# Two cross attentions on one core: scores computed two tiles ahead instead of three, exponentials moved to the head of ScalarE's step

## The reference

```
x = x + cross_attention_0(layernorm(x), ctx)
x = x + quantised_ffn(layernorm(x))
x = x + cross_attention_1(layernorm(x), ctx)   # with LoRA, and 4 tokens with keys and values of their own
x = x + mixture_of_experts(layernorm(x))       # 8 experts, top 2
```

## Time and profile before

| What | us |
|---|---|
| Median of 3 runs | 1635.89 |
| Lowest and highest | 1633.92, 1649.41 |
| The profiled execution, its own time | 1650.75 |
| Its span, first to last instruction | 1649.0 |
| First attention, first norm to last statistics | 90.3 to 314.4 |
| Second attention, first norm to last statistics | 819.5 to 1058.1 |

### The profile page before, as it was taken

How to read it: one execution, slowest core, us unless ns; L and a number is a source line. 1 busy time by engine, 2 the same in 40 slices (tenths; PEclk the granted TensorE clock), 3 DMA queues, 4 the chain that set the end, 5 groups by cost and what they waited for, 6 DMA issues and landing times. The chain is left out here.

```text
span 1649.0 us, 29274 instructions
## 1 busy us (share of the span) xinstructions
PE 1289.7 (78%) x8795; PEld 955.6 (58%) x8796; DVE 1064.8 (65%) x1954; ACT 796.7 (48%) x1146; POOL 522.8 (32%) x427
## 2 busy tenths in 40 slices
PE   5859999538986009799879999663079999999996
PEld 3427777434432008646446767553068999899995
DVE  4947777585589875544758888662346666665663
ACT  0536565244499777100567878563034334443342
POOL 1037777200000000100066767347403323333333
PEclk9979999868999559855899999855589999999998
DMA  5000000100033542100013222374323222222221
GB/s 196 1 4 1 0 0 0 58 1 1 0 150 136 204 158 68 40 1 0 23 45 91 64 89 64 92 251 156 113 62 53 37 51 46 45 47 44 47 43 12
DMA packets 62636, 102.67 MB, mean 62 GB/s; under 512 B 9648, under 2 KB 50704, under 8 KB 61936
## 3 DMA queue, kind: packets, MB, share of 16 engines
q1 hardware_dynamic: 48272, 84.98, 15.8%
q0 software_dynamic: 14304, 16.93, 5.7%
HBM read 65.79 MB, written 37.92 MB: 63 GB/s over the span
## 5 line engine op out<-in xcount | busy, mean ns | idle before, releaser
L1876 POOL DMA_INDIRECT out<-ex_yo,ex_mt x78 | 136.3, 1747 | 316.0 <-DVE ex_yo L1851 181.6
L1753 PE MATMUL ex_ps_h<-ex_xT_hi,a_arena 128*128 128x256 f16 x1248 | 212.4, 274 | 0.0
L1795 ACT ACTIVATE ex_hT<-ex_ps_h,e_b1T,e_unscale 128x256 f32<-128x256 f32 x312 | 150.8, 564 | 115.4 <-PE ex_ps_h L1753 115.4
L609 PE MATMUL at_ps_y<-c_VW,at_pT_hi 128*128 (+1 forms) x1024 | 172.3, 274 | 1.3 <-DVE main_x_res L736 1.3
L1753 PE MATMUL ex_ps_h<-ex_xT_lo,a_arena 128*128 128x256 f16 x624 | 170.9, 274 | 0.0
L1766 PE MATMUL ex_ps_y<-e_w_lo,ex_hT_hi 128*128 x624 | 170.1, 273 | 0.0
L1766 PE MATMUL ex_ps_y<-a_arena,ex_hT_lo 128*128 x624 | 170.1, 273 | 0.0
L1766 PE MATMUL ex_ps_y<-a_arena,ex_hT_hi 128*128 x624 | 170.1, 273 | 0.0
L811 POOL TENSOR_TENSOR at_sc<-at_sc,at_ri 128x960 f32<-128x960 f32 (+1 forms) x96 | 127.5, 1342 | 86.9 <-DVE at_ri L731 86.6
L811 POOL TENSOR_TENSOR at_sc<-at_sc,at_mx 128x960 f32<-128x960 f32 (+1 forms) x96 | 127.4, 1342 | 44.2 <-DVE at_mx L708 44.0
L609 PE MATMUL at_ps_y<-c_VW,at_pT_lo 128*128 (+1 forms) x512 | 140.0, 273 | 0.0
(11 more groups left out here) (295 smaller groups left out, 2982.0 us busy)
## 6 DMA issues: line engine op xcount, KB each, us to landing
at_half<-in_L_ffn_W SPq DMA_DIRECT2D x32, 512.0 KB, 4.3
up_scratch<-gm_stg SPq DMA_DIRECT2D x16, 768.0 KB, 3.2
gm_stg<-up_scratch SPq DMA_DIRECT2D x16, 768.0 KB, 4.2
ex_row<-xs SPq DMA_DIRECT2D x39, 260.0 KB, 2.7
rt_stage<-in_L_ffn_W SPq DMA_DIRECT2D x16, 512.0 KB, 4.2
main_x_res<-in_x SPq DMA_DIRECT2D x8, 512.0 KB, 12.7
out<-main_x_res SPq DMA_DIRECT2D x4, 1024.0 KB, 12.5
xs<-rt_pad SPq DMA_DIRECT2D x18, 130.0 KB
```

The lines of the kernel that those rows point to most:

```text
L609: last = nc.tensor.matmul(ps_y[:, 0:D], a[j][:, n, :], b[:, bass.ds(off + n * D, D)], start=(n == 0 and i == 0), stop=(n == NP - 1 and i = ...
L1753: last = nc.tensor.matmul(ps_h[:, n, :], a[:, bass.ds(e * WN + d * HID + n * P, P)], b[:, d, :], start=(m == 0), stop=(m == 3 * DT - 1))
L1795: last = nc.scalar.activation(hT[:, n, :], ps_h[:, n, :], ACT.Relu, bias=b1T[:, bass.ds(e * HT + n, 1)], scale=unscale[:, 0, bass.ds(e, 1)])
L1876: nc.gpsimd.indirect_dma_start(out=acc[:, :], out_offset=bass.IndirectOffsetOnAxis(ap=mt[j][:, q, 1:2].bitcast(U32), axis=0), in_=yo[j][:, ...
```

## The change

In the attention function, on all engines, the scores (with take_scores, maxima and subtract) are made two tiles ahead of the step's probabilities, not three, and the turn of x, norm, high_x, rest_x and add_bias three ahead, not four. The lead passed to `in_steps_by` goes from 4 to 3. On ScalarE `exps` goes from a place behind `high_p` (for tile k + 2) to the head of the step (for tile k + 1). Sums, inverses, normalise, turn_probs, high_p, rest_p, output, residual and statistics keep their indices. The counts that `column_sums` and `total` wait for follow. It applies to both attentions.

```
@@ TensorE
-                need(pe, xhi_r, NS * e + 7 if not isinstance(e, int) else min(NS * e + 7, NT))
-                need(pe, xlo_r, NS * e + 7 if not isinstance(e, int) else min(NS * e + 7, NT))
+                need(pe, xhi_r, NS * e + 6 if not isinstance(e, int) else min(NS * e + 6, NT))
+                need(pe, xlo_r, NS * e + 6 if not isinstance(e, int) else min(NS * e + 6, NT))
...
-                if there(k + 3, NT):
-                    scores(k + 3, (j + 3) % 2)
+                if there(k + 2, NT):
+                    scores(k + 2, j % 2)
                 if experts_w and j == 3 and there(k, NT):
                     column_sums(k // NS)
-                if there(k + 4, NT):
-                    turn_x(k + 4, j % 2)
+                if there(k + 3, NT):
+                    turn_x(k + 3, (j + 1) % 2)
...
-            in_steps_by(nc.tensor, NT, 4, 1, NS, step)
+            in_steps_by(nc.tensor, NT, 3, 1, NS, step)
@@ ScalarE
-                if there(k + 4, NT):
-                    norm(k + 4, j % 2)
+                if there(k + 1, NT):
+                    exps(k + 1, (j + 1) % NS)
                 if there(k + 3, NT):
-                    take_scores(k + 3, (j + 3) % NS)
-                if there(k + 4, NT):
-                    high_x(k + 4, j % 2)
+                    norm(k + 3, (j + 1) % 2)
+                if there(k + 2, NT):
+                    take_scores(k + 2, (j + 2) % NS)
+                if there(k + 3, NT):
+                    high_x(k + 3, (j + 1) % 2)
                 if there(k, NT):
                     high_p(k, j % 2)
-                if there(k + 2, NT):
-                    exps(k + 2, (j + 2) % NS)
                 if experts_w and there(k, NT):
                     weights(k // NS, j)
...
-            in_steps_by(nc.scalar, NT, 4, 0, NS, step)
+            in_steps_by(nc.scalar, NT, 3, 0, NS, step)
@@ VectorE
-                if there(NS * e + 7, NT):
-                    dve.wait_ge(xhi_r, NS * e + 8)
+                if there(NS * e + 6, NT):
+                    dve.wait_ge(xhi_r, NS * e + 7)
...
-                if there(k + 3, NT):
-                    maxima(k + 3, (j + 3) % NS)
+                if there(k + 2, NT):
+                    maxima(k + 2, (j + 2) % NS)
...
-                if there(k + 4, NT):
-                    rest_x(k + 4, j % 2)
+                if there(k + 3, NT):
+                    rest_x(k + 3, (j + 1) % 2)
...
-            in_steps_by(nc.vector, NT, 4, 2, NS, step)
+            in_steps_by(nc.vector, NT, 3, 2, NS, step)
@@ POOL
                 if there(k + 1, NT):
                     normalise(k + 1, (j + 1) % NS)
+                if there(k + 2, NT):
+                    subtract(k + 2, (j + 2) % NS)
                 if there(k + 3, NT):
-                    subtract(k + 3, (j + 3) % NS)
-                if there(k + 4, NT):
-                    add_bias(k + 4)
+                    add_bias(k + 3)
...
-            in_steps_by(nc.gpsimd, NT, 4, 0, NS, step)
+            in_steps_by(nc.gpsimd, NT, 3, 0, NS, step)
```

## The result

| | before | after |
|---|---|---|
| Median of 3 runs, us | 1635.89 | 1672.93 |
| Lowest and highest | 1633.92, 1649.41 | 1672.83, 1674.77 |
| Profiled execution, us | 1650.75 | 1674.77 |
| First attention, first norm to end of last statistics | 90.31 to 314.40, 224.1 | 90.05 to 328.11, 238.1 |
| Between the two | 505.1 | 504.5 |

The ratio of the medians is 1.021 (95% interval 1.012 to 1.029, so 20 to 48 us): slower by 37.0 us. The forecast was 1675. The two attentions became longer by 14.0 and 25.4, 39.4 together; 39.1 had been worked out. Some executions of one and the same kernel take 12 to 15 us longer (of the 22 of the kernel before beside experiments 3, 6, 7 and 8 two took 1648.61 and 1649.02, the others 1633.62 to 1637.97), and of before the 1649.41 and the profiled execution are such.

What follows compares the result with a forecast made beforehand. A closed loop through POOL's order was taken to replace TensorE's 6.30 us step as the bound; +13.4 (first attention) and +25.7 (second) sum to +39.1 on 1635.9, giving 1675 us, range 1655 to 1700.

Steps and rivals of the forecast that it cites:

- The ring: Both attentions: closed loop from one tile's subtract to the next's; 6.85 us a step in the first, 0.55 over TensorE's step.
- 0.12 for both: In the loop: releases POOL to ScalarE and ScalarE to VectorE cost 0.12 us together, with 0 and 0.28 as ends.
- First attention: +13.4 predicted: First attention: last exponentials 15.5 us later, at 315.6; the tail of 12.2 behind them gives back 2.1.
- I cost it at nothing: TensorE's clock: low stretches behind seven long gaps lose 1.8 us of work each, covered by slack in the following steps.
- low clock inside the attentions: Sign that would show the forecast wrong: a low TensorE clock within the attentions in the profile after.
- Second attention: +25.7 predicted: Second attention: rounds of four steps take 30.98 us instead of 27.29; last exponentials +28.1, with 2.4 given back behind them.
- the price is in the loop already: ScalarE: norm and turn_x are waited for behind the exponentials' new wait, but add nothing beyond the loop's length.
- TensorE's wait for norm: First attention: TensorE waits about 0.55 us a step for norm ahead of each turn_x, the whole excess, once.
- The clock as a rival: Second attention: TensorE at low clock a whole step behind seven long gaps, +28, in all +67, 1703 us; 8 in 100.
- The table load: First attention: the exponentials' table load of 1.28 us falls into idle time before the first exps; otherwise 1.3 us once.
- it lies in nothing that I changed: Base: the 15 us between profiled execution and the other runs' median lies outside the changed code; forecast uses the median.
- The fallback: First attention: if the loop vanished, the two-step chain of 12.64 us would remain, 6.32 a step, no cost.

Runs made afterwards that it cites:

- experiment 3: Changed kernel with two extra 128 x 128 additions on POOL in each step, behind add_bias: 1677.08 us in one run.
- experiment 6: The change in the first attention only, the second as in the kernel before: ratio 1.0075 to the kernel before.
- experiment 7: Changed kernel with only ScalarE's norm moved, to tile k+4 behind high_p: 1682.24 us in one run.
- experiment 8: Changed kernel with POOL's subtract ahead of normalise and norm moved to tile k+4 behind high_p: median 1644.06 us, ratio 1.0062 to the kernel before.
- experiment 1: Changed kernel with POOL's subtract put ahead of its normalise: median 1654.92 us, ratio 1.0065 to the kernel before.
- experiment 2: Changed kernel with normalise on eight of the 16 heads only, for timing alone as results differ: 1641.63 us in one run.
- experiment 4: Kernel before, scores still three ahead, with exps(k+2) moved to the head of ScalarE's step, ahead of norm: 1654.70 us in one run.
- experiment 9: Kernel before, scores still three ahead, with exps(k+2) moved to second place of ScalarE's step, behind norm(k+4): ratio 1.0008 to the kernel before.
- experiment 5: Changed kernel with exps(k+1) moved back behind high_p(k) on ScalarE, POOL as in the change: 1905.81 us in one run.

## Why the prediction was right

**The ring.** "subtract(t), exps(t), sums(t) and inverses(t), normalise(t), subtract(t+1)" is the bound: 6.77 measured, 6.85 predicted. Experiments 1 and 2 open and shorten it and the step falls to 6.35 to 6.38 and 6.30; experiments 3 and 7 change POOL's load and norm's place and it stays 6.76. The terms: exps to sums 1.19 (1.17 and a release had been put in), sums to normalise 1.78 as taken, normalise to subtract 1.86 (1.88 taken), subtract to exps 1.94. The last is 1.90 and a release of 0.04, and that of ScalarE to VectorE is within 0.04 too: 0.12 for both was on the high side of what came out, near the lower end that had been kept.

**First attention: +13.4 predicted, +14.0 measured,** but two terms were mis-sized and cancel: that the sum came so close is luck. The last exponentials came at 312.23, not 315.6, mostly because the ring is 0.08 shorter over 28 tiles. The tail behind them was to be 12.2 and took 15.9. Turn_probs came 4.92 behind the exponentials, as said; then the transposes took 1.97 instead of the 0.87 that I had put in. The rows of the two are from the timeline and the windows (columns as above):

```profile
317.15 1.97 PE L598 MATMUL at_ps_p<-main_ident,at_sc 128*128 128x128 f32 x8 [3.05 <-POOL at_sc L811]
```

```profile
316.00:318.00 2.00, 0.85 (x4) 0.85 (x5) 1.08 (x3) 0.00 (x0) 1.10 (x1) 0.53 0.00 0
318.00:320.00 2.00, 2.00 (x12) 1.63 (x11) 0.90 (x2) 1.20 (x2) 0.00 (x0) 0.50 0.00 0
```

TensorE had been idle for 3.05 us in front of turn_probs, because the distance of two leaves it nothing else to do at the end, and the clock then stood at its 1.2 GHz level for some six microseconds. Before, it stayed at 1.00 through this tail. "I cost it at nothing" holds for the steps and not for the tails. Experiments 3 and 7 give the price, as they have the same steps and the same gap of 3.05 there: with about half as much low clock the tail took 14.4, with none 13.1. So 2.8 of the 3.7 us are the clock, and the first attention is 11.1 us longer than before where the clock stays up (experiment 7), 14.0 where it falls. The "low clock inside the attentions" was one of the prediction's own signs of being wrong; it came, in the tails alone.

**Second attention: +25.7 predicted, +25.4 measured.** The steps came as worked out: 8.35, 7.83, 7.27 and 7.27 for 8.42, 7.88, 7.34 and 7.34, each 0.05 to 0.07 shorter for the releases, and 30.73 for 30.98. Counted from the first norm, the last exponentials came 26.3 later than before, where 28.1 had been worked out; the tail was 15.1 for 13.5, behind a gap of 3.43 with the clock at 0.50 (in experiment 3, behind the same gap at 1.00, it took 13.4). Here too two misses cancel. How the +25 is made up: opening POOL's ring gives back 16.1 (experiment 1). The 9.3 that stay have the step of 8.36 in them, in which high_w stands between two exponentials. The prediction had that step, at 8.42, beside the ring. Norm behind the exponentials, which costs 9.8 with scores three ahead (experiments 4 and 9), gives nothing back with two ahead (experiments 7 and 8), as "the price is in the loop already" said.

**TensorE's wait for norm.** Foretold as "0.55 a step, the whole excess". The rows say 0.24 for the matmul and 0.73 for its weight load, and the step is 0.46 longer. As a sign it was right; experiment 7 shows that it was never the cause, as the argument by the ring had said.

**The clock as a rival.** It would have put TensorE at the low level for a whole step behind each long gap. Behind the gaps of 1.33 and 1.82 read above it was at 1.00. The two tails had it low behind 3.05 and 3.43, but the length of a gap does not settle it. The same places in experiment 7 (first tail) and experiment 3 (second tail, where L598 is L600), with the stretch behind each:

```profile
329.49 1.09 PE L598 MATMUL at_ps_p<-main_ident,at_sc 128*128 128x128 f32 x8 [3.05 <-POOL at_sc L811]
```

```profile
330.00:332.00 2.00, 2.00 (x21) 1.83 (x20) 1.13 (x2) 1.09 (x2) 0.00 (x0) 1.00 0.00 0
```

```profile
1089.45 1.09 PE L600 MATMUL at_ps_p<-main_ident,at_sc 128*128 128x128 f32 x8 [3.43 <-POOL at_sc L813]
```

```profile
1090.00:1092.00 2.00, 2.00 (x20) 1.83 (x19) 1.17 (x2) 1.09 (x2) 0.00 (x0) 1.00 0.00 0
```

In experiment 5 it was low behind 3.18 and at 1.00 behind 3.10 one step on (207.68). The Trainium skill, "TensorE: Matmul & The Clock Gate", section "HAM oscillation — how this bites in real kernels", lets each burst behind such a wait start slow. That did not happen in the steps of this kernel; it happened in the two tails and in every second step of experiment 5's first attention, and not in the two places above.

**The table load** at the first exponentials was to be hidden, and was: it starts at 99.04 and takes 1.28, and the exponentials start at 102.00, where POOL releases them.

**The base.** Sum and median are to be set against each other with care. The profiled executions differ by 24.0: +14.0, +25.4, -0.6 between the attentions and -14.5 behind them, in code that the change does not touch. The stretch behind the second attention took 590.9 in the profiled run of before and 574.9 to 585.0 in all the others. Such time can lie elsewhere too: in the profiled runs of experiments 1 and 7 the first norm came at 102.8 and 102.5, in all the others at 89.6 to 91.0. What makes it was not found. That "it lies in nothing that I changed" fits these lengths, and taking it out of the base was right; 1635.9 + 39.4 is 1675.3, and 1672.93 was measured.

**The fallback** of 6.32 a step for the chain over two steps, should the ring vanish: experiment 1 had 6.35 to 6.38, experiment 2 6.30.

## What to carry to other kernels

Before work is moved closer together across engines, follow each item from its first instruction round to the same instruction of the next item, through every queue order, and add up the durations: a ring longer than the bounding engine's step is the new step, and no share of busy time shows it. An engine that is a third busy (POOL) can be in that ring by order alone. Then work of its own outside the ring costs next to nothing (experiment 3), while turning round two of its instructions (a step of 6.76 becomes 6.35) or shortening the one inside the ring (6.30) counts. When an instruction is put at the head of a queue, look for the one behind it that somebody waits for already, here norm, and keep that one in front.

## What the runs showed that had not been expected

- The place of one instruction decides between 6.8 and 9.5 to 11.1 us a step: with scores two tiles ahead, the exponentials behind high_p close a ring through the low part of x (1905.81 us in all, experiment 5).
- The same gap of TensorE can leave the granted clock at either level: behind 3.05 us it was 0.53 in the kernel after and 1.00 in experiment 7, behind 3.43 it was 0.50 and, in experiment 3, 1.00; behind 2.19 it was 0.59 in the kernel before, behind 2.23 (at 896.37 in experiment 7) 1.00. What decides was not found. In the first tail it is worth 2.8 us.
- A release from POOL to ScalarE costs 0.04 us (208.90 + 1.90 to 210.84), less than the 0.14 from VectorE to ScalarE in rows 5.
